# Softplus written to delta's buffer in SBUF, and DVE's product with u reading it there

## The chip, the cores and the metric

The kernel runs on one core of a Trainium2 chip. The metric is the device time of the whole program on that core, in microseconds. A core has five engines with queues of their own: PE (matmuls), DVE (VectorE), ACT (ScalarE), POOL (GpSimd) and SP, which here only issues DMAs. They meet at semaphores. PE writes only to PSUM; POOL works on SBUF alone.

## What is computed

Eight images of 96x64x64 go through a layer with a state-space block (two-dimensional selective scan), two convolutions with channel attention, an attention layer and a quantized feed-forward layer. Nearly all the time goes to the selective scan, with K = 4 directions, D_INNER = 192 channels, 16 states per channel and 4096 positions:

```python
def selective_scan(xs, dts, A, Bs, Cs, Ds, dt_bias):
    delta = jax.nn.softplus(dts + dt_bias[None, :, :, None])
    ...
    def step(h, inp):
        u_t, d_t, b_t, c_t = inp
        dA = jnp.exp(d_t[..., None] * A)
        h = dA * h + (d_t * u_t)[..., None] * b_t[:, :, None, :]
        y = jnp.einsum('bkdn,bkn->bkd', h, c_t)
        return (h, y)
    _, ys = jax.lax.scan(step, h0, (u_l, d_l, B_l, C_l))
    y = jnp.moveaxis(ys, 0, -1)
    return y + Ds[None, :, :, None] * xs
```

The change touches `delta` (the softplus) and `d_t * u_t`, its product with u, which the kernel calls `du`.

## The kernel before

For each of the eight images the program runs a stage that prepares the inputs (`prep`: norms, projections, depthwise convolution), the scan stage, and a stage for the rest (`post`). The scan stage takes about 1160 us of an image's 1530.

**How the scan is cut.** The 4 x 192 rows of channels are laid out as T = 0 to 5, each with 128 partitions: T = 0 and 3 walk the image by rows, T = 1 and 4 by columns, and T = 2 and 5 hold the remaining 64 channels of both ways. Each T has 4 chunks of 1024 positions. So an image has 24 chunks g, each with n = 0 to 15 steps, one for each state: 384 steps. All tiles of a step are 128x1024, f32. Below, "chunk (1, 2)" is T = 1 with its third chunk, counted from 0.

**A step**, engine by engine (the lines are those of the profile):

- ACT computes exp(delta * A) into `decay` (into a PSUM tile `pb` for n in `POOLED` = 3, 7, 11, 15), L1199, and copies the last column of a finished state into `carry`, L1143.
- DVE runs the scan, L1278, over 1024 positions. In 8 of 16 steps it first multiplies B, spread over the partitions in PSUM by PE (L1015), by `du`, L1265. In the 4 steps of `POOLED`, POOL makes that product from SBUF, L1298, and in the 4 steps of `TURNS` = 1, 5, 9, 13 ACT (L1186) and PE (L1056, transposes) do.
- POOL multiplies the state by C, L1309, in place; PE adds the sixteen up in PSUM, L1065. POOL has 16 + 4 instructions of 128x1024 in a chunk.

The order on each engine is written out by hand: each engine has a function `steps` that walks the steps of a chunk, with constants such as `SOFTPLUS_AT` that say behind which step the work for the following chunk stands. Every engine works through its queue in order.

**delta of the following chunk.** Within chunk g, PE computes the pre-activation of g + 1 into the PSUM tile `pc` after step 1 (`pre_dt`). ACT turns it into delta at step 2 (`softplus`, L1149, in place in `pc`, between two loads of ACT's tables). DVE reads `pc` and u at step 5 and writes `du` (`next_du`, L1245; L1283 is the same for the first chunk of a stage). At step 7 ACT copies `pc` to `delta` in SBUF (`delta_out`, L1157). Then `pc` is used again: PE turns B in it (`turn_b`, step 8, L1040), ACT takes that out, and PE turns `du` in it (`turn_du`, step 11, L1048). In chunks of T = 1 and 4, u is read by columns, with a stride of 64 elements (`chunk`).

`du` and `delta` have two buffers each, by the parity of g. All of `u`, `du`, `delta`, `decay`, `state`, `c_sb` and `b_sb` lie in SBUF; `pb`, `pc` and `py` in PSUM.

## Time and profile before

| | us |
|---|---|
| median of 3 runs (12321.95 to 12329.25) | 12322.18 |
| the profiled execution | 12312.74 |
| its span, first to last instruction | 12310.8 |
| DVE busy | 10864.5 (88%) |
| PE busy | 10629.6 (86%) |
| POOL busy | 9515.3 (77%) |
| ACT busy | 8817.2 (72%) |

The profile is of one execution. "Busy" is the time in which an engine has an instruction running; the shares are means over stages that differ: in the scan stage DVE and POOL are busy nearly all the time, and in `post` POOL has little to do. A view of groups gives, for each line of the kernel, how often its instruction ran, its mean duration, and how long the engine had sat idle just before it. A timeline gives single instructions with their start. Consecutive instructions of an engine overlap by 0.04 to 0.09 us in these records, so durations and starts are to be read together.

### The profile page before, as it was taken

To read this page: it belongs to the slowest core of one execution; us is meant where nothing else is said; L and a number is where in the kernel's file an instruction comes from. 1 tells how busy PE (TensorE), PEld (TensorE's weight loads), DVE (VectorE), ACT (ScalarE), POOL (GpSimd) and SP (SyncE) were. 2 spreads that over 40 slices of the span, in tenths; PEclk is the share of its full clock that TensorE was granted. 3 is DMA by queue.
4 is the path that set the end of the run, shared out by engine and by line. 5 is a ranking of instruction groups with operands and counts; after the bars stand their busy time and mean duration, and the time that the engine had idled before them with its cause. 6 is when DMAs were issued, how large, how long until landed. Compare 5 with 4: busy or idle time off the path is not lost. (4 is left out here: it accounts for less than half of the span.)

```text
span 12310.8 us, 117469 instructions
## 1 busy us (share of the span) xinstructions
PE 10629.6 (86%) x33046; PEld 4749.1 (39%) x33046; DVE 10864.5 (88%) x7695; ACT 8817.2 (72%) x18292; POOL 9515.3 (77%) x4213
## 2 busy tenths in 40 slices
PE   7888888888888888888888888888888888888888
PEld 2443334343344433434334443334433344334443
DVE  7999779997799978999789997899968999689996
ACT  5777667776677766777667776677766777667776
POOL 4999459994599945999459994599936999369993
PEclk9999989999899998999989999999998999999999
DMA  4677446764467644677446774477745677356773
GB/s 140 214 222 214 117 133 215 221 215 110 134 214 222 214 109 139 215 221 214 104 143 215 221 214 101 148 215 219 214 97 149 216 220 215 94 153 215 219 215 91
DMA packets 677497, 2203.72 MB, mean 179 GB/s; under 512 B 165008, under 2 KB 167056, under 8 KB 665424
## 3 DMA queue, kind: packets, MB, share of 16 engines
q1 hardware_dynamic: 676848, 2196.22, 61.3%
q8 instruction: 266, 4.36, 0.2%
q14 instruction: 383, 3.14, 0.1%
HBM read 2098.86 MB, written 67.11 MB: 176 GB/s over the span
## 5 line engine op out<-in xcount | busy, mean ns | idle before, releaser
L1309 POOL TENSOR_TENSOR state<-state,c_sb 128x1024 f32<-128x1024 f32 x3072 | 7180.7, 2363 | 610.5 <-ACT carry L1143 528.5
L1065 PE MATMUL ps<-state,wt 128*128 128x512 f32 x12288 | 5863.5, 614 | 350.5 <-ACT ya L1136 233.4
L1278 DVE TENSOR_TENSOR_SCAN state<-decay,carry,ps 128x1024 f32<-128x1024 f32 x1728 | 4006.7, 2340 | 41.1
L1065 PEld LDWEIGHTS ps<-state,wt 128*128 128x128 f32 x12288 | 2324.5, 196 | 2778.8 <-issue 2105.3
L1199 ACT ACTIVATE decay<-delta,a_neg 128x1024 f32<-128x1024 f32 x2304 | 2638.6, 1146 | 0.2 <-issue 0.2
L1186 ACT ACTIVATE dbu_t<-du_t,b_t 128x128 f32<-128x128 f32 (+1 forms) x8128 | 2301.4, 360 | 0.0
L1143 ACT COPY carry<-state 128x1 f32<-128x1 f32 x3072 | 572.0, 186 | 2136.4 <-DVE state L1278 2127.1
L1265 DVE TENSOR_TENSOR ps<-ps,du 128x1024 f32<-128x1024 f32 x1544 | 1866.2, 1209 | 97.9 <-PE ps L1015 97.6
L1298 POOL TENSOR_TENSOR dbu<-b_sb,du 128x1024 f32<-128x1024 f32 x768 | 1811.5, 2359 | 0.0
L1015 PE MATMUL ps<-parts,sel 114*128 114x512 bf16 (+1 forms) x3088 | 944.7, 388 | 679.6 <-DVE state L1278 673.1
L1278 DVE TENSOR_TENSOR_SCAN state<-ps,carry,dbu 128x1024 f32<-128x1024 f32 x576 | 1343.2, 2332 | 68.1 <-ACT ps L1199 47.6
L1278 DVE TENSOR_TENSOR_SCAN state<-decay,ps 128x1024 f32<-128x1024 f32 x576 | 1301.9, 2280 | 13.6
L1056 PE MATMUL ps<-wt,dbu_t 128*128 128x128 f32 x6080 | 812.5, 276 | 184.0 <-ACT dbu_t L1186 177.4
L1056 PEld LDWEIGHTS ps<-wt,dbu_t 128*128 128x128 f32 x6080 | 683.2, 141 | 627.6 <-issue 434.3
L1199 ACT ACTIVATE ps<-delta,a_neg 128x1024 f32<-128x1024 f32 x768 | 854.4, 1113 | 0.0
L1015 PEld LDWEIGHTS ps<-parts,sel 114*128 114x128 bf16 (+1 forms) x3088 | 218.6, 97 | 1529.4 <-DVE state L1278 1309.7
L1625 POOL CAST h<-h16b 128x1536 fp8e5<-128x1536 f16 x64 | 116.0, 1812 | 896.0 <-DVE h16b L1750 896.0
L307 ACT ACT_TABLE_LOAD x409 | 524.7, 1283 | 71.4 <-DMA x_tok<-x 27.1
L1278 DVE TENSOR_TENSOR_SCAN state<-ps,dbu 128x1024 f32<-128x1024 f32 x192 | 436.3, 2272 | 29.2 <-ACT ps L1199 16.0
L507 ACT ACTIVATE rs<-ps,wt 96x512 f32<-96x512 f32 (+1 forms) x320 | 218.7, 683 | 314.5 <-PE ps L492 171.9
L1611 POOL TENSOR_TENSOR sqa<-sqa,sqr 64x512 f32<-64x512 f32 x64 | 100.9, 1577 | 402.2 <-ACT sqr L1519 402.2
L1027 PE MATMUL ps<-parts,dt_w 114*128 114x512 bf16 (+1 forms) x1536 | 377.7, 389 | 30.3 <-PEq L664 30.3
(218 smaller groups left out, 9959.1 us busy)
## 6 DMA issues: line engine op xcount, KB each, us to landing
c_sb<-bc SPq DMA_DIRECT2D x2048, 512.0 KB, 4.6
c_sb<-bc SPq DMA_DIRECT2D x2048, 256.0 KB, 5.7
b_sb<-bc SPq DMA_DIRECT2D x512, 512.0 KB, 4.1
b_sb<-bc SPq DMA_DIRECT2D x512, 256.0 KB, 4.0
x_nat<-x SPq DMA_DIRECT2D x17, 1536.0 KB, 14.8
gates<-gate_a SPq DMA_DIRECT2D x8, 2048.0 KB, 6.8
x_tok<-x SPq DMA_DIRECT2D x288, 48.0 KB, 1.9
gn<-gn_t SPq DMA_DIRECT2D x8, 1536.0 KB, 7.1
```

Source lines behind the costliest of these rows:

```text
L307: act.add_instruction(mybir.InstLoadActFuncSet(name=nc.get_next_instruction_name(), act_func_set_id=which, ins=[], outs=[]))
L1015: mm = pe.matmul(bank[:, q * CH:(q + 1) * CH], sel[own, n, first:first + 128], part_cols(at, 2 * (T // 3), q, own), start=True, stop=True)
L1027: mm = pe.matmul(pc[:, q * CH:(q + 1) * CH], dt_w[own, p, w, :], part_cols(at, k, q, own), start=(i == 0 and p == 0), stop=(i == len(ways) ...
L1056: mm = pe.transpose(pb[n % 2][:, j * 128:(j + 1) * 128], dbu_t[:, j, :], col("ident"))
L1065: mm = pe.matmul(py[:, q * CH:(q + 1) * CH], col("ident"), state[:, slot(g, n), q * CH:(q + 1) * CH], start=(n == 0), stop=False)
L1143: act.copy(carry[:, n:n + 1], state[:, slot(g, n), last:last + 1]).then_inc(S["carried"], 1)
L1186: last = act.activation(dbu_t[:, j, o * wide:(o + 1) * wide], du_t[:, j, o * wide:(o + 1) * wide], ACT.Copy, scale=b_t[:, g % 2, j, i:i + 1])
L1199: act.activation(pb[n % 2][:, :] if n in POOLED else decay[:, n % 2, :], delta[:, g % 2, :], ACT.Exp, scale=a_neg[:, T, n:n + 1]).then_inc ...
L1265: dve.tensor_tensor(pb[n % 2][:, :], pb[n % 2][:, :], du[:, g % 2, :], ALU.mult)\
L1278: dve.tensor_tensor_scan(state[:, slot(g, n), way], rate, what, 0.0 if fresh else carry[:, n:n + 1], ALU.mult, ALU.add)\
L1298: pool.tensor_tensor(dbu[:, i % BRING, :], b_sb[:, i % BRING, :], du[:, g % 2, :], ALU.mult)\
L1309: pool.tensor_tensor(state[:, slot(g, n), :], state[:, slot(g, n), :], c_sb[:, n % CRING, :], ALU.mult).then_inc(S["weighted"], 1)
```

## The change

The softplus writes to `delta` in SBUF and no longer to `pc`; `next_du` reads `delta` there; `delta_out`, ACT's copy, and its semaphore `delta_ready` are gone. Who waited for `delta_ready` now waits for `delta_made`. The softplus waits for the readers of the buffer that it overwrites, two chunks back, and `turn_du` waits for `du_ready` itself.

```diff
@@ -1031,7 +1031,7 @@
                     def turn_b(T, at, g):
 
-                        pe.wait_ge(S["delta_ready"], g + 1)
+                        pe.wait_ge(S["delta_made"], g + 1)
...
@@ -1044,6 +1044,7 @@
                     def turn_du(g):
 
                         pe.wait_ge(S["bt_out"], g + 1)
+                        pe.wait_ge(S["du_ready"], g + 1)
...
@@ -1146,15 +1147,12 @@
 
                         tables(act, SOFTPLUS_SET)
                         act.wait_ge(S["pre_mm"], g + 1)
-                        act.activation(pc[:, :], pc[:, :], ACT.Softplus, bias=col("dt_b", 128, T))\
+                        if g > 1:
+                            act.wait_ge(S["decayed"], (g - 1) * NS)
+                            act.wait_ge(S["du_ready"], g - 1)
+                        act.activation(delta[:, g % 2, :], pc[:, :], ACT.Softplus, bias=col("dt_b", 128, T))\
                            .then_inc(S["delta_made"], 1)
                         ln_exp_tables(act)
-
-                    def delta_out(g):
-
-                        act.wait_ge(S["du_ready"], g + 1)
-                        act.wait_ge(S["decayed"], max(g - 1, 0) * NS)
-                        act.copy(delta[:, g % 2, :], pc[:, :]).then_inc(S["delta_ready"], 1)
...
@@ -1203,8 +1201,6 @@
                                 if n == SOFTPLUS_AT:
                                     softplus(following[0], g + 1)
-                                if n == DELTA_AT:
-                                    delta_out(g + 1)
...
                     softplus(0, 0)
-                    delta_out(0)
                     b_out(0, 0)
...
@@ -1242,7 +1237,7 @@
                         dve.wait_ge(S["dbu_pooled"], (g - 1) * NP + CREDIT)
                         if g > 1:
                             dve.wait_ge(S["dut_mm"], g - 1)
-                        dve.tensor_tensor(like(du[:, g % 2, :], T), like(pc[:, :], T), u_of(T, at), ALU.mult)\
+                        dve.tensor_tensor(like(du[:, g % 2, :], T), like(delta[:, g % 2, :], T), u_of(T, at), ALU.mult)\
                            .then_inc(S["du_ready"], 1)
...
                     dve.wait_ge(S["delta_made"], 1)
-                    dve.tensor_tensor(du[:, 0, :], pc[:, :], u_of(0, 0), ALU.mult).then_inc(S["du_ready"], 1)
+                    dve.tensor_tensor(du[:, 0, :], delta[:, 0, :], u_of(0, 0), ALU.mult).then_inc(S["du_ready"], 1)
```

ACT's queue at the head of a scan stage, before the change: L1149 is the softplus, L1157 the copy to `delta`, L1163 takes the turned B out of `pc`, L1172 the turned `du`, L1199 is the first exponential.

```order
L307 ACT_TABLE_LOAD
L1149 ACTIVATE ps<-ps,wt 128x1024
L307 ACT_TABLE_LOAD
L1157 COPY delta<-ps 128x1024
L1163 COPY b_t<-ps 128x8x4
L1172 COPY du_t<-ps 128x1024
L1199 ACTIVATE decay<-delta,a_neg 128x1024 x2
```

And after it:

```order
L307 ACT_TABLE_LOAD
L1153 ACTIVATE delta<-ps,wt 128x1024
L307 ACT_TABLE_LOAD
L1161 COPY b_t<-ps 128x8x4
L1170 COPY du_t<-ps 128x1024
L1197 ACTIVATE decay<-delta,a_neg 128x1024 x2
```

The copy between the second table load and the copy of B is gone; in the same way it goes from behind step 7 of each later chunk, with nothing else moved.

DVE's queue in the first chunk, from step 3 to step 6, before (scans are printed with the operation's other name; `du` of the following chunk is L1245):

```order
L1278 SCALAR_TENSOR_TENSOR state<-ps,dbu 128x1024
L1265 TENSOR_TENSOR ps<-ps,du 128x1024
L1278 SCALAR_TENSOR_TENSOR state<-decay,ps 128x1024
L1245 TENSOR_TENSOR du<-ps,ua 128x1024
L1278 SCALAR_TENSOR_TENSOR state<-decay,ps 128x1024
```

And after:

```order
L1273 SCALAR_TENSOR_TENSOR state<-ps,dbu 128x1024
L1260 TENSOR_TENSOR ps<-ps,du 128x1024
L1273 SCALAR_TENSOR_TENSOR state<-decay,ps 128x1024
L1240 TENSOR_TENSOR du<-delta,ua 128x1024
L1273 SCALAR_TENSOR_TENSOR state<-decay,ps 128x1024
```

Nothing moves here; the product has the same place, and its first input is `delta` in SBUF where it was a tile of PSUM.

## Rows read from the trace of the kernel before

**Rows 1.** Page, costliest groups: busy, mean ns, idle before, and its causes

```profile
L1278 DVE TENSOR_TENSOR_SCAN state<-decay,carry,ps 128x1024 f32<-128x1024 f32 x1728 | 4006.7, 2340 | 41.1
```

**Rows 2.** Busy time by engine, scan stage of the second image, T = 0

```profile
core 0: us, PE busy (x) PEld busy (x) DVE busy (x) ACT busy (x) POOL busy (x), PEclk, DMA share, GB/s
1725.00:1905.00 180.00, 156.84 (x498) 68.07 (x498) 176.13 (x95) 131.93 (x266) 172.56 (x75) 0.92 0.67 217
```

**Rows 3.** The product `du`, whole program: duration ns min/median/max, first and last start

```profile
L1245 DVE TENSOR_TENSOR du<-ps,ua x120: 1198/1898/1943, 207.6 to 11805.6; 128x1024 f32<-128x1024 f32 x120
L1245 DVE TENSOR_TENSOR du<-ps,ur x64: 1201/1225/1226, 546.3 to 12001.2; 128x1024 f32<-128x1024 f32 x64
```

**Rows 4.** Timeline of `post`, DVE and POOL: start us, us, instruction [idle before]

```profile
1374.42 0.74 DVE L1650 SCALAR_TENSOR_TENSOR ya<-ya,wt,gate_a 128x512 f32<-128x512 f32 x1
1374.43 1.85 POOL L1611 TENSOR_TENSOR sqa<-sqa,sqr 64x512 f32<-64x512 f32 x1 [5.01 <-ACT sqr L1519]
1375.09 1.74 DVE L1653 SCALAR_TENSOR_TENSOR yrc<-yrc,wt,gate_r 64x512 f32<-64x512 f32 x1
...
1381.28 1.82 DVE L1641 SCALAR_TENSOR_TENSOR yrc<-yrc,wt,rs 64x512 f32<-64x512 f32 x1
1381.29 1.25 POOL L1611 TENSOR_TENSOR sqa<-sqa,sqr 64x512 f32<-64x512 f32 x1 [5.01 <-ACT sqr L1519]
```

**Rows 5.** Timeline of `prep`, the end of POOL's share of the convolution

```profile
121.68 1.27 POOL L720 TENSOR_TENSOR conv_acc<-conv_acc,conv_tap 128x512 f32<-128x512 f32 x1
...
122.77 0.49 DVE L848 TENSOR_SCALAR conv_acc<-pad_r,wt 128x512 f32<-128x512 f32 x1
...
123.04 1.35 POOL L720 TENSOR_TENSOR conv_acc<-conv_acc,conv_tap 128x512 f32<-128x512 f32 x1
```

**Rows 6.** Timeline, five chunks of the second image: POOL's instruction and DVE's `du`

```profile
1783.45 2.34 POOL L1309 TENSOR_TENSOR state<-state,c_sb 128x1024 f32<-128x1024 f32 x1
1785.18 1.20 DVE L1245 TENSOR_TENSOR du<-ps,ua 128x1024 f32<-128x1024 f32 x1
...
1830.76 2.34 POOL L1309 TENSOR_TENSOR state<-state,c_sb 128x1024 f32<-128x1024 f32 x1
1832.93 1.20 DVE L1245 TENSOR_TENSOR du<-ps,ua 128x1024 f32<-128x1024 f32 x1
...
2026.05 2.37 POOL L1309 TENSOR_TENSOR state<-state,c_sb 128x1024 f32<-128x1024 f32 x1 [0.18 <-ACT carry L1143]
2026.07 1.93 DVE L1245 TENSOR_TENSOR du<-ps,ua 128x1024 f32<-128x1024 f32 x1 [0.32 <-PE ps L1056]
...
2074.94 2.36 POOL L1309 TENSOR_TENSOR state<-state,c_sb 128x1024 f32<-128x1024 f32 x1 [0.19 <-ACT carry L1143]
2075.53 1.23 DVE L1245 TENSOR_TENSOR du<-ps,ur 128x1024 f32<-128x1024 f32 x1 [0.89 <-PE ps L1056]
...
2171.82 2.36 POOL L1309 TENSOR_TENSOR state<-state,c_sb 128x1024 f32<-128x1024 f32 x1 [0.57 <-ACT carry L1143]
2172.91 1.23 DVE L1245 TENSOR_TENSOR du<-ps,ur 128x1024 f32<-128x1024 f32 x1
```

**Rows 7.** Waits of the program (us in total, times, longest); POOL at a step 8

```profile
POOL state L1309 <- ACT carry L1143: 528.5, 457, 30.8
...
1942.44 2.35 POOL L1309 TENSOR_TENSOR state<-state,c_sb 128x1024 f32<-128x1024 f32 x1 [0.93 <-ACT carry L1143]
```

**Rows 8.** Timeline, head of the second image's scan stage: ACT, DVE and PE

```profile
1713.67 1.09 ACT L1149 ACTIVATE ps<-ps,wt 128x1024 f32<-128x1024 f32 x1 [0.56 <-PE ps L1027]
...
1714.79 1.23 DVE L1283 TENSOR_TENSOR du<-ps,ua 128x1024 f32<-128x1024 f32 x1 [3.38 <-ACT ps L1149]
...
1716.07 1.01 ACT L1157 COPY delta<-ps 128x1024 f32<-128x1024 f32 x1
...
1717.78 1.97 PE L1048 MATMUL ps<-wt,du 128*128 128x128 f32 x8 [0.28 <-ACT b_t L1163]
```

**Rows 9.** DVE with two inputs in SBUF, and with one in PSUM: ns min/median/max

```profile
L514 DVE TENSOR_TENSOR cen<-cen,rs x128: 671/679/689, 59.3 to 12184.2; 96x512 f32<-96x512 f32 x128
...
L497 DVE TENSOR_TENSOR cen<-x,ps x192: 669/682/685, 1386.2 to 12288.6; 96x512 f32<-96x512 f32 x192
```

More of the change, by code:

```diff
@@ L66 @@
 BLOCKS = 8
-PRE_AT, SOFTPLUS_AT, DU_AT, DELTA_AT = 1, 2, 5, 7
+PRE_AT, SOFTPLUS_AT, DU_AT = 1, 2, 5
 BT_AT, BT_OUT_AT, DUT_AT, DUT_OUT_AT = 8, 10, 11, 13
@@ L277, in build @@
         gn_stored gates_ready gates_stored conv_mm conv_taps u_ready conv_r conv_p conv_sum ur_ready
-        ur_in xp_mm xp_hi xp_out xp_rest xp_mid xp_low parts_zero bc_stored parts_in pre_mm delta_made delta_ready du_ready b_mm decayed dbu_ready
+        ur_in xp_mm xp_hi xp_out xp_rest xp_mid xp_low parts_zero bc_stored parts_in pre_mm delta_made du_ready b_mm decayed dbu_ready
         dbu_pooled scanned carried weighted summed y_summed y_taken c_in_0 c_in_1 c_in_2 c_in_3 b_in_0
@@ L1196, in steps @@
                             if n == 0:
-                                act.wait_ge(S["delta_ready"], g + 1)
+                                act.wait_ge(S["delta_made"], g + 1)
                             act.wait_ge(S["scanned"], g * NS + n - 1 + CREDIT)
```

## The prediction

> **What bounds the kernel now.** I read the page's groups first. DVE's scans are the largest work that must run in order: 1728 of the 3072 take 2340 ns each, and DVE sat idle before them for 41.1 us in the whole program [rows 1]. So in the scan stage DVE is the engine that sets the time. The table by stretch says it again and adds the second thing to see: of 180 us, DVE is busy 176.13 and POOL 172.56 [rows 2]. POOL is only 3.6 us behind DVE, its instructions follow each other nearly without a gap, and any moment at which DVE starts something finds POOL in the middle of an instruction. ACT (131.93) and PE are not the bound [rows 2]. Whatever is added to DVE's queue in the scan stage comes out at the end; what is taken from ACT there does not, unless DVE was waiting for ACT.
>
> The third view is where the change has its cost: what happens when a DVE instruction with both inputs in SBUF meets a POOL instruction. In the scan stage of before there is none: each product, scan and `du` has one input in PSUM. In `post` there is. At 1374.42 DVE starts L1650, both inputs in SBUF, and POOL's L1611 starts 0.01 us behind it. POOL takes 1.85 us, where the same instruction takes 1.25 at 1381.29 [rows 4]: it was held for 0.60, the time in which DVE streamed its 512 elements. Then DVE's L1653 starts at 1375.09, beneath POOL's instruction, and takes 1.74 us where its twin L1650 took 0.74. It ends at 1376.83, 0.55 after POOL's end at 1376.28. At 1381.28 the same once more: L1641 takes 1.82, ending at 1383.10, 0.56 behind POOL's end at 1382.54 [rows 4]. So the two do not share: the later waits until the earlier is through. For 512 elements, 0.55 us is about the streaming alone (0.74 less some 0.18 of start, which lay under POOL's tail).
>
> The Trainium skill has the rule, in "SBUF — State Buffer", section "Who interferes with whom": a DVE instruction with two SBUF inputs reads the second through an interface that it shares with GpSimd, and whichever comes second blocks fully. The trace agrees (1.74 for 0.74).
>
> **The change, part by part.**
>
> *1. `du` from SBUF.* 184 products [rows 3] (23 per image; the first of each stage, L1283, comes when POOL has nothing to do) now have two SBUF inputs, in the middle of POOL's work. Each pays what is left of POOL's current instruction, less a start-up of about 0.12 us (0.68 of an instruction of this kind [rows 9], less the 0.55 that is left of it behind POOL's end [rows 4]). The remainder can be read off, since each chunk of a kind meets POOL in nearly the same phase. From the timeline of the second image, POOL's start plus its time less DVE's start:
> - 3 chunks per image, (1, 1), (1, 2) and (4, 2): both start together, 2026.05 + 2.37 - 2026.07 = 2.35 us [rows 6];
> - 2 chunks, (1, 3) and (4, 3): 2074.94 + 2.36 - 2075.53 = 1.77;
> - 5 chunks, (2, 1) to (2, 3), (5, 1) and (5, 2): 2171.82 + 2.36 - 2172.91 = 1.27;
> - 5 chunks, (0, 1), (2, 0), (3, 0), (3, 1), (5, 0): 0.32 to 0.61, mean 0.46; the 0.61 is 1783.45 + 2.34 - 1785.18;
> - 7 chunks, (0, 2), (0, 3), (1, 0), (3, 2), (3, 3), (4, 0), (4, 1): 0.16 to 0.31, mean 0.21; 1830.76 + 2.34 - 1832.93 = 0.17;
> - 1 chunk, (0, 0): POOL idle, nothing.
>
> Sum: 3 x 2.35 + 2 x 1.77 + 5 x 1.27 + 5 x 0.46 + 7 x 0.21 = 7.05 + 3.54 + 6.35 + 2.30 + 1.47 = 20.7; less 22 x 0.12 = 2.6 gives 18.1 us per image, **145 us** in eight. It is on the path: behind `du` stand scan 5 and all later steps on DVE, and no wait follows that it could fill (see 3).
>
> Does POOL's next instruction, right behind the current one, get in first? The nearest row is in `prep`: DVE's L848 starts at 122.77 under a POOL instruction that ends at 122.95. POOL's next, which follows at once, starts at 123.04 and takes 1.35 in place of 1.27, and DVE is through at 123.26 [rows 5]. So DVE came in between two adjoining POOL instructions. I take one wait per product, not two.
>
> *2. The product itself.* SBUF in place of PSUM: 679 ns with both inputs in SBUF, 682 with one in PSUM [rows 9]. Taken at 0. For T = 1 and 4 the 1.90 us come from reading u by columns [rows 3], which stays. Another page of the Trainium skill, "VectorE: DVE Perf Modes", section on the TRN2 errata, gives a fixed 120 cycles to a PSUM source and 58 to an SBUF one; as an estimate from it, 0.065 us x 184 would be 12 us less. The rows show 3 ns, so it is not in my sum.
>
> *3. POOL held.* While DVE streams, POOL stands: about 1.08 us (1.20 less 0.12) for 15 products of an image, and 1.8 for the 8 with a stride. But DVE has lost the remainder too, so relative to DVE POOL falls back by 1.08 less the remainder: ahead at 1.27, back 0.9 at 0.17, and 1.6 in the strided chunks with a short remainder. POOL waits for ACT's carry 528.5 us in the program, of which the openings of eight stages are 30 each [rows 7]: 290 us in 192 chunks, 1.5 in each, mostly at steps 6 and 8, soon after `du` (0.93 at one step 8 [rows 7]). That covers it, and because POOL meets DVE again at step 8, the phases above should come back in the next chunk. Taken at 0; if that cover is gone, POOL's 15 x 1.08 + 8 x 1.8 = 31 us per image is the price, 245 in all, less the 145 that DVE pays already.
> Late in chunks of T = 2 and 5 DVE waits a little for POOL and PE, which now have had more time. Between 0 and 20 us; I take **-7**.
>
> *4. The copy goes.* 1.01 us of ACT [rows 8], 184 times in the loop. ACT has 48 of 180 us free [rows 2] and waits there for DVE's scans: 0. At the head of a stage it is on the path: ACT's copy from 1716.07 to 1717.08, then PE's `turn_b`, ACT's copy of B, and `turn_du` at 1717.78 [rows 8]. Now `turn_b` runs on PE under the table load, `du` ends at 1716.02, and `turn_du` can start near 1716.3. That is 1.45 us (between 1.01, the copy, and 1.75), eight times: **-12**.
>
> *5. The softplus.* It reads PSUM and writes SBUF; the copy L1157 does that in 1.01, the softplus into PSUM takes 1.09 [rows 8]. Between -0.08 and +0.08 on a piece of ACT's queue for which DVE waits at step 3: 15 us at most either way, taken at 0. Its new waits are for work a chunk back and long done; `turn_du`'s wait for `du_ready`, at step 11, is for step 5. PE's and SP's queues don't move.
>
> Sum: 145 - 7 - 12 = +126 us. On the profiled execution, 12312.7 + 126 = 12439; the median lies 9.4 above that execution, so 12448.
>
> **The rivals.**
> - *Ties fall to DVE.* In the three chunks with 2.35 us both engines start within 0.02 us. Of the pairs in rows 4, DVE had the earlier start both times, won one and lost one. If DVE wins these: 3 x 2.2 x 8 = 53 us less, 12395. Still slower.
> - *The phases drift, or POOL becomes the bound.* If POOL's hold shifts it so that DVE meets it at random, the remainder is half of 2.34, 1.17 less 0.12, times 184: 193 us; if half of POOL's hold that DVE has not paid comes on top, some 50: up to 12322 + 240 = 12562. For it: POOL has 1.5 us of slack against a hold of 1.8 in the strided chunks. Against: it waits at both steps 6 and 8 there.
> - *POOL's next instruction does get in first.* Then each of the 10 longest cases per image pays 2.3 more, 184 us: about 12630. Rows 5 speak against it; there DVE's instruction is of another kind, though.
> - *No conflict* (faster or level, the other side of the forecast): the block is for the pair in `post`, or the second input of this `tensor_tensor` isn't read through what POOL uses. Then only the head's 12 us, and up to 15 of the softplus, are left: 12295 to 12320, at 12308 within 0.2%. It decides at one place, `du`'s duration beside a POOL instruction: 1.20 or up to 3.5 us. Rows 4 speak against it plainly, with instructions that read SBUF as both do here.
>
> **How the numbers follow.** Forecast as worked out, the ties either way: 0.65. Drift or POOL as bound: 0.15. Two waits per product: 0.05. No conflict: 0.15, of which a quarter ends faster by over 0.2%. A measurement of this kernel can tell about 0.2% (25 us) from no change, so: faster 0.04, same 0.12, slower 0.84. Range: from 12370, below the ties' 12395 for the term of the softplus, to 12565, the drifting case's end; outside lie the case without conflict and the one with two waits, 0.2.
>
> **What would show it.** In the profile of the changed kernel: `du` (now L1240) takes 1.20 to 3.5 us for an unstrided input, mean about 0.8 above before's, and ends some 1.1 us (1.8 strided) behind the end of the POOL instruction that it met. POOL's instruction behind it takes up to 1.1 or 1.8 us longer or starts later. Scan 5 follows at once. The copy of 1.01 us is gone from ACT and ACT's idle time grows by as much. The first scan of a stage comes about 1.45 us earlier. If `du` stays at 1.20 and 1.90 everywhere, step 1 is wrong; if it is right but the total is off by over 50 us, step 3 is (phases, POOL's slack): POOL's wait at step 8 would have gone.

## The result, and the profile after

The changed kernel takes **12474.85 us** (median, 12463.19 to 12493.39), the kernel before 12322.11 (12321.95 to 12329.25): a ratio of 1.0124, 95% interval 1.0106 to 1.0141, so 1.2% slower. The forecast was 12448, from 12370 to 12565. The profiled executions are 12463.19 and 12312.74 us long, their spans 12461.3 and 12310.8: 150.5 us more.

Nearly all of it stands in the busy time of one instruction. The view of groups, kernel after (line, engine, operation, count, busy us, mean ns, idle before and its cause):

```profile
L1240 DVE TENSOR_TENSOR du<-delta,ua 128x1024 f32<-128x1024 f32 x120 | 273.1, 2276 | 11.8 <-PE ps L1057 11.8
L1240 DVE TENSOR_TENSOR du<-delta,ur 128x1024 f32<-128x1024 f32 x64 | 145.4, 2273 | 35.1 <-PE ps L1057 33.6
```

The same groups of the kernel before:

```profile
L1245 DVE TENSOR_TENSOR du<-ps,ua 128x1024 f32<-128x1024 f32 x120 | 190.2, 1585 | 12.5 <-PE ps L1056 12.5
L1245 DVE TENSOR_TENSOR du<-ps,ur 128x1024 f32<-128x1024 f32 x64 | 78.4, 1224 | 35.1 <-PE ps L1056 33.9
```

273.1 + 145.4 less 190.2 + 78.4 is 149.9 us. In single instructions (min/median/max ns), where [rows 3] had 1198/1898/1943 and 1201/1225/1226:

```profile
L1240 DVE TENSOR_TENSOR du<-delta,ua x120: 1199/1930/6553, 206.5 to 11949.8; 128x1024 f32<-128x1024 f32 x120
L1240 DVE TENSOR_TENSOR du<-delta,ur x64: 1515/2352/2885, 552.2 to 12148.5; 128x1024 f32<-128x1024 f32 x64
```

The page says how little else moved. The scan takes 2340 ns as before and DVE's idle time before it is 48.5 us (41.1 in [rows 1]). POOL's L1304 now waits 461.5 us for the carry (528.5 in [rows 7]), and its instructions take 2416 ns on average, with the times in which they are held:

```profile
L1304 POOL TENSOR_TENSOR state<-state,c_sb 128x1024 f32<-128x1024 f32 x3072 | 7344.5, 2416 | 566.0 <-ACT carry L1144 461.5
...
L1273 DVE TENSOR_TENSOR_SCAN state<-decay,carry,ps 128x1024 f32<-128x1024 f32 x1728 | 4007.8, 2340 | 48.5 <-PE ps L1057 7.4
```

ACT is busy 8650.2 us by the page, instead of 8817.2: the copies are gone, and nobody was waiting for them. In the table by stretch for T = 0 of the second image, which answers to [rows 2], DVE remains the engine with nearly no idle time (175 of 180 us):

```profile
1745.00:1925.00 180.00, 150.54 (x476) 65.03 (x477) 175.06 (x91) 123.41 (x253) 168.11 (x72) 0.92 0.66 210
```

**How one product waits.** The timeline of the second image, for the chunks of [rows 6]: start, duration, engine, instruction, idle time before. The first DVE row in each piece is `du`, the POOL row beside it is the instruction that it met, the next POOL row the one behind.

```profile
1858.55 1.26 DVE L1240 TENSOR_TENSOR du<-delta,ua 128x1024 f32<-128x1024 f32 x1
...
1856.38 2.34 POOL L1304 TENSOR_TENSOR state<-state,c_sb 128x1024 f32<-128x1024 f32 x1
...
2104.16 2.88 DVE L1240 TENSOR_TENSOR du<-delta,ur 128x1024 f32<-128x1024 f32 x1 [0.87 <-PE ps L1057]
...
2103.60 2.36 POOL L1304 TENSOR_TENSOR state<-state,c_sb 128x1024 f32<-128x1024 f32 x1 [0.17 <-ACT carry L1144]
...
2203.53 2.35 DVE L1240 TENSOR_TENSOR du<-delta,ur 128x1024 f32<-128x1024 f32 x1
...
2202.44 2.36 POOL L1304 TENSOR_TENSOR state<-state,c_sb 128x1024 f32<-128x1024 f32 x1 [0.68 <-ACT carry L1144]
...
2204.76 3.32 POOL L1304 TENSOR_TENSOR state<-state,c_sb 128x1024 f32<-128x1024 f32 x1
```

Read the third, chunk (2, 1). POOL's instruction ends at 2204.80, 1.27 us after `du` starts. `du` ends at 2205.88, 1.08 behind that, so of its 2.35 us 1.14 were waiting. POOL's next starts in the records at 2204.76, takes 3.32 in place of 2.36, and ends when it would have ended had it begun behind `du`'s reading. In chunk (1, 3) 1.80 is left and `du` takes 2.88 (1.08 behind POOL's end again); in (0, 2) 0.17 is left and it takes 1.26.

Two pieces are not of that form. In chunk (1, 1) both start together (POOL at 2003.62, for 2.37 us), and POOL was first: `du` takes 4.13, its normal 1.92 and 2.21 of waiting. In (1, 2) both start together, and DVE was first: `du` takes its normal 1.92, and POOL's instruction 4.13.

```profile
2003.63 4.13 DVE L1240 TENSOR_TENSOR du<-delta,ua 128x1024 f32<-128x1024 f32 x1 [0.31 <-PE ps L1057]
...
2054.72 1.92 DVE L1240 TENSOR_TENSOR du<-delta,ua 128x1024 f32<-128x1024 f32 x1 [0.29 <-PE ps L1057]
...
2054.72 4.13 POOL L1304 TENSOR_TENSOR state<-state,c_sb 128x1024 f32<-128x1024 f32 x1 [0.17 <-ACT carry L1144]
```

And in chunk (0, 1) `du` takes 6.25 us. With 0.57 of POOL's instruction left it lets not only that one go by, but the two behind it, and gets in only when POOL has nothing more to do:

```profile
1804.41 6.25 DVE L1240 TENSOR_TENSOR du<-delta,ua 128x1024 f32<-128x1024 f32 x1
...
1802.63 2.35 POOL L1304 TENSOR_TENSOR state<-state,c_sb 128x1024 f32<-128x1024 f32 x1
...
1804.93 2.35 POOL L1304 TENSOR_TENSOR state<-state,c_sb 128x1024 f32<-128x1024 f32 x1
...
1807.24 2.34 POOL L1293 TENSOR_TENSOR dbu<-b_sb,du 128x1024 f32<-128x1024 f32 x1
```

I call this a lost turn below: a POOL instruction that began after `du` had, and read first.

### The profile page after: what moved, and what is told of

Its sections match the earlier page's. It is cut to its first block and busy times, and to the rows that moved or that the text cites. A ratio compares the mean times of both kernels' runs of the same rounds, so it can differ in the third digit from the quotient of the medians.

```text
span 12461.3 us, 117445 instructions
## 1 busy us (share of the span) xinstructions
PE 10691.9 (86%) x33046; PEld 4774.9 (38%) x33046; DVE 11017.6 (88%) x7695; ACT 8650.2 (69%) x18100; POOL 9711.9 (78%) x4213
## 5 line engine op out<-in xcount | busy, mean ns | idle before, releaser
L1304 POOL TENSOR_TENSOR state<-state,c_sb 128x1024 f32<-128x1024 f32 x3072 | 7344.5, 2416 | 566.0 <-ACT carry L1144 461.5
L1066 PE MATMUL ps<-state,wt 128*128 128x512 f32 x12288 | 5916.8, 618 | 350.6 <-ACT ya L1137 233.7
L1273 DVE TENSOR_TENSOR_SCAN state<-decay,carry,ps 128x1024 f32<-128x1024 f32 x1728 | 4007.8, 2340 | 48.5 <-PE ps L1057 7.4
L1066 PEld LDWEIGHTS ps<-state,wt 128*128 128x128 f32 x12288 | 2344.4, 197 | 2803.3 <-issue 2123.9
L1293 POOL TENSOR_TENSOR dbu<-b_sb,du 128x1024 f32<-128x1024 f32 x768 | 1839.7, 2395 | 0.0
L1015 PE MATMUL ps<-parts,sel 114*128 114x512 bf16 (+1 forms) x3088 | 954.1, 391 | 792.5 <-DVE state L1273 788.3
L1057 PE MATMUL ps<-wt,dbu_t 128*128 128x128 f32 x6080 | 819.2, 277 | 168.9 <-ACT dbu_t L1184 163.4
L1057 PEld LDWEIGHTS ps<-wt,dbu_t 128*128 128x128 f32 x6080 | 689.0, 142 | 612.1 <-issue 414.0
L1015 PEld LDWEIGHTS ps<-parts,sel 114*128 114x128 bf16 (+1 forms) x3088 | 219.6, 98 | 1644.9 <-DVE state L1273 1415.0
```

What stands on the lines that cost most here:

```text
L1015: mm = pe.matmul(bank[:, q * CH:(q + 1) * CH], sel[own, n, first:first + 128], part_cols(at, 2 * (T // 3), q, own), start=True, stop=True)
L1057: mm = pe.transpose(pb[n % 2][:, j * 128:(j + 1) * 128], dbu_t[:, j, :], col("ident"))
L1066: mm = pe.matmul(py[:, q * CH:(q + 1) * CH], col("ident"), state[:, slot(g, n), q * CH:(q + 1) * CH], start=(n == 0), stop=False)
L1273: dve.tensor_tensor_scan(state[:, slot(g, n), way], rate, what, 0.0 if fresh else carry[:, n:n + 1], ALU.mult, ALU.add)\
L1293: pool.tensor_tensor(dbu[:, i % BRING, :], b_sb[:, i % BRING, :], du[:, g % 2, :], ALU.mult)\
L1304: pool.tensor_tensor(state[:, slot(g, n), :], state[:, slot(g, n), :], c_sb[:, n % CRING, :], ALU.mult).then_inc(S["weighted"], 1)
```

## The experiments

The question was whether the 150 us are what the prediction says: `du` pays, from SBUF and only from SBUF, what is left of POOL's instruction at the place where it meets it.

### The same order with one input moved: PSUM against SBUF

The first pair has the same instructions at the same places and differs in one operand. In both, ACT's copy of delta stands at step 5, `du` behind it at step 6. Two waits follow from that order, in both alike: the first product of a stage now waits for ACT's copy, and `turn_b` waits for `du`. The kernel is otherwise the one before. In the first `du` reads `pc` in PSUM, in the second `delta` in SBUF.

```diff
-PRE_AT, SOFTPLUS_AT, DU_AT, DELTA_AT = 1, 2, 5, 7
+PRE_AT, SOFTPLUS_AT, DU_AT, DELTA_AT = 1, 2, 6, 5
...
-                        act.wait_ge(S["du_ready"], g + 1)
+                        act.wait_ge(S["delta_made"], g + 1)
...
-                        dve.wait_ge(S["delta_made"], g + 1)
+                        dve.wait_ge(S["delta_ready"], g + 1)
```

and in the second also:

```diff
-                        dve.tensor_tensor(like(du[:, g % 2, :], T), like(pc[:, :], T), u_of(T, at), ALU.mult)\
+                        dve.tensor_tensor(like(du[:, g % 2, :], T), like(delta[:, g % 2, :], T), u_of(T, at), ALU.mult)\
```

> The kernel before with two moves: ACT's copy of delta to SBUF at step 5 (it was at 7), and du at step 6 (it was at 5), still with pc in PSUM as its first input. Partner of e2_sbuf_at6, which differs from it in that input alone. Theory (a DVE instruction with two SBUF inputs and a POOL instruction exclude each other): du takes 1.20 to 1.23 us, and 1.9 with the stride, in all 184 cases; the time is that of the kernel before but for what the moved copy costs DVE: 12310 to 12360 us. Rival (what costs time in the changed kernel is the earlier or moved work on ACT, or du's place): this kernel is slower than before by 100 us or more.

> As e1_psum_at6, with delta in SBUF as the first input of du, and nothing else changed (the same waits, the same copy on ACT). Theory: each du pays the rest of POOL's running instruction less 0.12 us. At step 6 of the trace of before that rest sums to 226 us over the 184 products (phases taken as they were with du at step 5; ties and POOL getting in first can add or take 50): 150 to 280 us over e1_psum_at6. Rival (the second SBUF input costs nothing; something else of the change does): within 25 us of e1_psum_at6. Second rival (the cost does not hang on POOL's phase but is a fixed price of the operand): 150 us, and du longer by the same amount in every chunk.

From PSUM: 12363.71 us (12344.9 to 12366.77), ratio to the kernel before 1.003 (1.0017 to 1.0042). From SBUF: 12597.58 (12590.65 to 12609.26), ratio 1.0224 (1.0209 to 1.024). Groups of `du`, from PSUM and then from SBUF:

```profile
L1248 DVE TENSOR_TENSOR du<-ps,ua 128x1024 f32<-128x1024 f32 x120 | 193.3, 1610 | 4.2
L1248 DVE TENSOR_TENSOR du<-ps,ur 128x1024 f32<-128x1024 f32 x64 | 78.4, 1224 | 2.2
```

```profile
L1248 DVE TENSOR_TENSOR du<-delta,ua 128x1024 f32<-128x1024 f32 x120 | 387.2, 3226 | 4.2
L1248 DVE TENSOR_TENSOR du<-delta,ur 128x1024 f32<-128x1024 f32 x64 | 109.8, 1715 | 2.2
```

The one operand costs 233.9 us in the medians and 497.0 - 271.7 = 225.3 us in `du`'s busy time. The same chunk, (0, 2) of the second image, in the timelines of the two:

```profile
1845.57 1.22 DVE L1248 TENSOR_TENSOR du<-ps,ua 128x1024 f32<-128x1024 f32 x1
...
1844.79 2.35 POOL L1301 TENSOR_TENSOR dbu<-b_sb,du 128x1024 f32<-128x1024 f32 x1
```

```profile
1882.45 2.65 DVE L1248 TENSOR_TENSOR du<-delta,ua 128x1024 f32<-128x1024 f32 x1
...
1881.65 2.36 POOL L1301 TENSOR_TENSOR dbu<-b_sb,du 128x1024 f32<-128x1024 f32 x1
...
1883.97 3.33 POOL L1312 TENSOR_TENSOR state<-state,c_sb 128x1024 f32<-128x1024 f32 x1
```

Both meet POOL's instruction with 1.57 and 1.56 us left. From PSUM `du` takes 1.22; from SBUF 2.65, and POOL's next is held to 3.33. So the second SBUF input is the cause, with nothing else changed (the first product of each stage reads the other source too, but POOL is idle there). The change under study does two things at once, since it also drops the copy; this pair has the copy in both. The remainders in the second kernel's own trace, each less 0.12, sum to 184 us, and 22 of its 184 products lost one turn, some 50 us more: 234 us together, against the 229 by which `du` is longer than undisturbed products are.

The first kernel came out 3.7 us above the upper end of what was expected of it. In it DVE waits 36 us more for others. 20 of them are at the head of the eight stages, where the first product waits for ACT's copy, 49.8 us in all, and had waited 29.6 for the softplus:

```profile
L1286 DVE TENSOR_TENSOR du<-ps,ua 128x1024 f32<-128x1024 f32 x8 | 9.8, 1224 | 49.8 <-ACT delta L1160 49.8
```

The rest is for PE: 14 us more for its sum (23.1 at L1066, where the kernel before has 8.8) and 12 more for its B (109.6 at L1015, where it has 97.6), with some 10 less elsewhere. That is a first sign that `du`'s place matters to more than the meeting with POOL.

### du at other steps

If each product pays the remainder at its place, the place sets the price. One line of the changed kernel is edited, with 4, 9 and 10 in turn:

```diff
-                    PRE_AT, SOFTPLUS_AT, DU_AT = 1, 2, 5
+                    PRE_AT, SOFTPLUS_AT, DU_AT = 1, 2, 9
```

> The changed kernel with du at step 9 (it was at 5), which is free now since pc is no longer held for it. At step 8 POOL waits for the carry in most chunks, so DVE finds it idle. Theory (the price of du is the rest of POOL's running instruction): read off the trace of before at step 9 the rests sum to 36 us; with du gone from step 5 POOL has 1.1 to 1.8 us less slack up to step 8, which gives some of it back. 12320 to 12400 us, and du's excess over 1.21 and 1.92 us sums to what the kernel has over 12310. Rival (a fixed price per product, or POOL's hold of 245 us is what costs): no better than the changed kernel, 12450 to 12490.

> The changed kernel with du at step 10, one step further. There POOL has just begun an instruction in nearly all chunks: the rests in the trace of before sum to 283 us. Theory: 12310 + 283 = 12590, 12530 to 12640, the slowest of all places so far although the code differs from e_du9 by one step. Rival (no dependence on POOL's phase): as e_du9 within 25 us.

> The changed kernel with du at step 4 (it was at 5). Theory: the rests of POOL's instruction at step 4 of the traces sum to 75 us (148 at step 5); and du now stands ahead of DVE's wait for the turned product of step 5, which is 56 us in the program and can take some of it in. 12310 + 75 - 56 = 12330, with the phases' uncertainty 12310 to 12400. Rival (a fixed price per product): 12450 less at most 56, 12395 to 12450. du's excess would tell: 60 to 110 us in sum against 150.

Measured: at 9 12513.89 us (12503.52 to 12529.81), ratio 1.0157 (1.014 to 1.0173); at 10 12805.62 (12780.01 to 12813.42), ratio 1.0389 (1.037 to 1.0407); at 4 12570.06 (12563.18 to 12578.33), ratio 1.0196 (1.0181 to 1.0211). All three totals were missed, every one by being slower. What `du` itself costs came as expected at 10 (283 us expected, 273 measured); at 9 the 36 us that had been read off became 68, and at 4 the 60 to 110 became 137. By its total the kernel with `du` at 9 came out as its rival had it, no better than the change; but the rival's reason, a fixed price per product, is ruled out by `du`'s own 68, 150 and 273 us at three places. Groups of `du`, at step 9 and then at step 10:

```profile
L1240 DVE TENSOR_TENSOR du<-delta,ua 128x1024 f32<-128x1024 f32 x120 | 232.0, 1933 | 0.0
L1240 DVE TENSOR_TENSOR du<-delta,ur 128x1024 f32<-128x1024 f32 x64 | 104.7, 1636 | 0.0
```

```profile
L1240 DVE TENSOR_TENSOR du<-delta,ua 128x1024 f32<-128x1024 f32 x120 | 381.1, 3176 | 4.2
L1240 DVE TENSOR_TENSOR du<-delta,ur 128x1024 f32<-128x1024 f32 x64 | 160.5, 2509 | 2.2
```

At 9 `du` is busy 336.7 us, at 10 541.6, against 268.6 in the kernel before: 68 and 273 us more, where the change has 150. The remainders of their own traces, less 0.12 each, sum to 64 and 259 us, the rest is lost turns (two in one product at 9, one each in eight products at 10). At 4 they sum to 69, but 30 products lost a turn, which makes 137. The account of DVE's time in the scan stage shows where the totals went. "Waits" is all that `du`, the products with B and the scans waited for other engines, summed over DVE's rows in the view of waits; the differences are to the kernel before (268.6 and 270.4 us, span 12310.8):

| `du` at | `du` busy | waits | sum | span |
|---|---|---|---|---|
| 5, the change | +150.0 | -1.5 | +148.5 | +150.5 |
| 9 | +68.1 | +104.9 | +173.0 | +190.9 |
| 10 | +273.1 | +191.1 | +464.2 | +500.8 |
| 4 | +136.5 | +104.6 | +241.1 | +257.5 |
| 6, PSUM | +3.0 | +35.8 | +38.8 | +51.5 |
| 6, SBUF | +228.3 | +36.3 | +264.6 | +278.0 |

The last two rows agree in their waits: these belong to the order (some 20 us to the head, as said above, the rest to the place) and not to the source. The sum leaves 2 to 37 us of the span's difference that I have not assigned. Who is waited for: DVE's waits (us in total, times, longest) with `du` at 9,

```profile
DVE ps L1260 <- PE ps L1015: 120.0, 121, 3.3
...
DVE state L1273 <- PE ps L1057: 106.7, 134, 2.8
...
DVE state L1273 <- PE ps L1066: 36.2, 48, 1.3
```

with `du` at 10, and PE's there,

```profile
DVE state L1273 <- PE ps L1057: 190.1, 187, 2.6
```

```profile
PE ps L1049 <- DVE du L1240: 362.6, 183, 4.4
```

and with `du` at 4:

```profile
DVE ps L1260 <- PE ps L1015: 132.2, 154, 3.3
DVE state L1273 <- PE ps L1066: 94.4, 125, 1.5
```

In the changed kernel the waits at L1015, L1057 (in scans) and L1066 are 84.0, 7.4 and 7.4. With `du` at 10, PE stands at `turn_du` (L1049, step 11) until `du` is there, 183 times, and what it owes DVE at step 13 comes late: 145 us of the 190.1 are there. With `du` at 9 that wait of PE is gone (2.7 us in all), yet by single records DVE waits 63 us at step 13, where it had waited next to nothing; the cause of that part stays open. The wait at step 5 is no part of the price: the wait for PE's turned product stands ahead of `du` in DVE's queue, and it is 45.3 us in the changed kernel (in `du`) and 43.5 with `du` at 9 (in the scan). What `du` at step 5 did cover lies behind it: at steps 7 and 8, PE's sum and PE's B cost 29 and 23 us more without it there. With `du` at 4, ahead of the wait at step 5, that wait is gone, and 87 us more for PE's sum and 33 for ACT's exponential at step 7, and 43 more for B at step 8, take its place. I had worked out the remainders only and taken PE as a cover that stays.

**The clock of TensorE moves too.** PE runs at one of two levels, 2.4 GHz, or 1.2 where a profile's PEclk reads 0.50; a matmul of L1066 takes 592 ns at the one and 1061 at the other (medians). In the scan stages the traces have 551 us at the lower level in the kernel before, 733 in the changed one, and 834, 1192 and 1226 with `du` at 9, 10 and 4. In the last, the second image has, besides 31 us at its head, such a stretch of 3.4 to 10.2 us in nearly every chunk. In one of them the clock fell just as PE came out of a wait of 2.46 us for ACT's copy of the finished sum, and DVE's scan at step 7 then waited 1.24 us for the sum:

```profile
2124.00:2127.00 3.00, 3.00 (x4) 1.12 (x4) 2.35 (x1) 2.50 (x7) 3.00 (x2) 0.50 0.14 52
...
2127.61 2.35 DVE L1273 TENSOR_TENSOR_SCAN state<-ps,carry,dbu 128x1024 f32<-128x1024 f32 x1 [1.24 <-PE ps L1066]
```

Of the 105 us more that DVE waits with `du` at 4, 78 are waits that ended at the lower level; with `du` at 9 and 10 it is 10 of 105 and 15 of 191. So at 4 the place and the clock cannot be told apart by these runs; at 9 and 10 little of what is waited stands in those stretches. In the changed kernel the waits that ended at the lower level are 62 us, where the kernel before has 73: the clock has no visible part in the 150.

### du at step 3 from PSUM, with the new head

Here the kernel before takes over only the head of the change: ahead of the first chunk the softplus goes to `delta`, and the first `du` reads it there. `du` of the other chunks, from PSUM, moves to step 3, where DVE waits 0.56 us on average for ACT's exponential in 113 of 192 chunks.

```diff
-PRE_AT, SOFTPLUS_AT, DU_AT, DELTA_AT = 1, 2, 5, 7
+PRE_AT, SOFTPLUS_AT, DU_AT, DELTA_AT = 1, 2, 3, 7
...
-                    softplus(0, 0)
-                    delta_out(0)
+                    act.sem_inc(S["delta_ready"], 1)
+                    tables(act, SOFTPLUS_SET)
+                    act.wait_ge(S["pre_mm"], 1)
+                    act.activation(delta[:, 0, :], pc[:, :], ACT.Softplus, bias=col("dt_b", 128, 0))\
+                       .then_inc(S["delta_made"], 1)
+                    ln_exp_tables(act)
...
-                    dve.tensor_tensor(du[:, 0, :], pc[:, :], u_of(0, 0), ALU.mult).then_inc(S["du_ready"], 1)
+                    dve.tensor_tensor(du[:, 0, :], delta[:, 0, :], u_of(0, 0), ALU.mult).then_inc(S["du_ready"], 1)
```

> A version that should beat both. The kernel before (du reads pc in PSUM, the copy at step 7 stays) with du at step 3, where DVE waits for the exponential that follows the softplus (79 us in the program at step 3, and 56 at step 5), and with the changed kernel's order at the head of a stage alone (softplus to delta, du reading it there, no copy; POOL is idle then): -12. Theory: du's 1.2 us go into those waits: up to -120, and the head -12: 12190. But in e_du9, where du was also gone from step 5, DVE waited some 0.5 us more per chunk for PE at steps 7 and 8; if that comes here too, 60 to 100 comes back. 12200 to 12300. Rival (PE is the bound behind step 5 and takes all of it): 12300 to 12330.

12339.49 us (12324.17 to 12346.39), ratio 1.0008 (0.9999 to 1.0017): no gain. DVE's waits for other engines, where the kernel before has 63.6 for ACT's L1199 at step 3, 46.4 for PE in `du`, and 8.8 for PE's sum:

```profile
DVE ps L1272 <- PE ps L1015: 106.6, 135, 3.3
DVE state L1285 <- PE ps L1067: 102.0, 115, 1.5
```

The wait at step 3 is gone entirely, and PE's sum at step 7 takes its place. What is saved ahead of that is handed back there. 58 of the 102 us are again waits that ended with PE at its lower clock (908 us of it in the scan stages, 551 in the kernel before). This is the rival that the expectation named, a few microseconds worse; whether PE's place or its clock is what hands the gain back was not separated.

### The new head alone

```diff
-                    softplus(0, 0)
-                    delta_out(0)
+                    act.sem_inc(S["delta_ready"], 1)
...
```

with the other lines of the head as above and `du` at step 5 from PSUM.

> The kernel before with the new head alone: before the first chunk of each image ScalarE's softplus goes straight to delta's buffer and the first product with u reads it there, so that the copy of delta is no longer ahead of TensorE's first transposes and matmuls; all other chunks keep softplus in PSUM and ScalarE's copy. This is the prediction's step 4 by itself. In the changed kernel the first product of an image follows du by 1.47 us less than before, 8 times, 11.8 us. If that is a gain and nothing behind it takes it back: 12305 to 12316, the ratio about 0.999, with DVE's time in du unchanged at about 269 us, since no other product of an image reads SBUF twice. If what comes behind (POOL's state products, which the first chunk waits for at its step 11) is the bound of the first chunk, it is taken back in that wait: 12318 to 12326 and longer waits of the scan at step 11.

12320.89 us (12311.24 to 12335.78) against 12327.8 (12318.01 to 12342.49) for the kernel before beside it: ratio 0.9993, interval 0.9985 to 1.0002. The sign is the expected one, the size (6.9 us of the 11.8) cannot be told from nothing. `du` stayed at 268.8 us (268.6). The head is shorter, as in the changed kernel; but the scan at step 11 of the first chunk, which waits for POOL, waits longer: 1.25 us instead of 0.73, by the gaps between DVE's records in the eight images, so about 4 of the 12 us come back there. Even this best version is not shown to beat the kernel before.

### Inputs exchanged

Does it matter which of the two SBUF inputs comes second?

```diff
-                        dve.tensor_tensor(like(du[:, g % 2, :], T), like(delta[:, g % 2, :], T), u_of(T, at), ALU.mult)\
+                        dve.tensor_tensor(like(du[:, g % 2, :], T), u_of(T, at), like(delta[:, g % 2, :], T), ALU.mult)\
```

> The changed kernel with the product's inputs exchanged: u first, delta second. If any second SBUF input excludes POOL whichever it is, du's excess is 150 us as in the changed kernel and the time 12460 to 12490. If it mattered which tile comes second (its address or its stride), the strided chunks of T = 1 and 4 would differ from the others, or the excess go away.

12461.89 us (12454.5 to 12472.91), ratio 1.0109 (1.0092 to 1.0126). The groups of `du`:

```profile
L1240 DVE TENSOR_TENSOR du<-ua,delta 128x1024 f32<-128x1024 f32 x120 | 265.5, 2212 | 11.4 <-PE ps L1057 11.4
L1240 DVE TENSOR_TENSOR du<-ur,delta 128x1024 f32<-128x1024 f32 x64 | 145.4, 2273 | 34.3 <-PE ps L1057 32.5
```

The same to the tenth of a microsecond for `ur`, and 8 us less for `ua`. There the three ties of an image fell to DVE in 24 of 24 cases here, in 19 of 24 in the changed kernel. And the strided products that wait only for a short remainder are 0.06 to 0.08 us shorter: 1.90 instead of 1.98 in chunk (0, 3), with 0.19 and 0.18 left. So the order of the inputs takes nothing off the wait that is worth having.

### Does a lost turn hang on the moment or on the chunk?

In the changed kernel chunk (0, 1) lost two turns in 7 of 8 images, with 0.56 to 0.61 us of POOL's instruction left, and (3, 0) two in one image, at 0.60. A fill by DVE, ahead of `du`, moves the moment: first of 128x128 in all chunks of T = 0 and 3, then of 128x480 in chunk (0, 1) alone.

```diff
+                            if n == DU_AT and after and T in (0, 3):
+                                dve.memset(idle_out[:, :], 0.0)
```

```diff
+                            if n == DU_AT and after and (T, c) == (0, 1):
+                                dve.memset(idle_out[:, :], 0.0)
```

> The changed kernel with a memset of 128x128, about 0.2 us, put on DVE ahead of du in the 8 chunks of T = 0 and 3 of each image. In the changed kernel the du of chunk (0, 1), which starts 0.56 to 0.61 us before the end of POOL's instruction, lost to POOL twice in 7 of 8 images and took 6.3 us; at 0.48 it was never lost, nor at 1.27. If the loss hangs on the moment, it goes: (0, 1) takes 1.2 + 0.3 us, some 4 us less per image, and the memset itself costs nothing where it shortens the wait by as much: 12322 + 150 - 31, 12420 to 12460. If it hangs on the chunk (its addresses, its queue), (0, 1) stays at 6.3 us and the time at 12470 to 12500.

> The changed kernel with one more fill of 128x480 values by DVE, ahead of the du that is executed in the second chunk of transform 0 alone (8 times in all). There du took 6.2 to 6.3 us in 8 of 8 images, with 0.46 of POOL's instruction left as well as with 0.60. The fill of 128x128 moved du by 0.14 us; this one should move it by about 0.5 us, so that it starts within 0.15 us of the end of POOL's instruction. If the two lost turns belong to starts with 0.4 to 0.6 us left: du takes about 1.3 us there and the whole is 8 x (5.07 - 0.5) = 37 us less than the changed kernel, 12430 to 12445. If they belong to this chunk, whatever the moment: du still takes 5.8 to 6.2 us and the time is 12465 to 12480. If du then comes after POOL's next one has begun: about 3.6 us for du, 12445 to 12460.

The first: 12479.77 us (12473.43 to 12489.88), ratio 1.0123 (1.0108 to 1.0138). The second: 12487.47 (12475.03 to 12509.48), ratio 1.0126 (1.011 to 1.0141). Chunk (0, 1) of the second image in the two timelines:

```profile
1816.17 6.16 DVE L1241 TENSOR_TENSOR du<-delta,ua 128x1024 f32<-128x1024 f32 x1
...
1814.27 2.36 POOL L1307 TENSOR_TENSOR state<-state,c_sb 128x1024 f32<-128x1024 f32 x1
```

```profile
1821.02 0.46 DVE L1266 MEMSET idle_out<- 128x480 f32 x1
1821.40 5.78 DVE L1241 TENSOR_TENSOR du<-delta,ua 128x1024 f32<-128x1024 f32 x1
...
1819.11 2.38 POOL L1307 TENSOR_TENSOR state<-state,c_sb 128x1024 f32<-128x1024 f32 x1
...
1821.42 2.37 POOL L1307 TENSOR_TENSOR state<-state,c_sb 128x1024 f32<-128x1024 f32 x1
...
1823.73 2.37 POOL L1296 TENSOR_TENSOR dbu<-b_sb,du 128x1024 f32<-128x1024 f32 x1
```

0.46 and 0.09 us are left now, and the two turns are lost in 8 of 8 images in both, as expected if the chunk decides (the second total is 7 us above the range for that case); `du` ends at the same place behind POOL's third instruction. In the changed kernel products that meet POOL with 0.44 to 0.48 left, in (2, 0), (3, 1) and (5, 0), lose none; with the first fill (3, 1) lost two turns in one image. So the moment alone does not decide. Nor does the chunk alone: (3, 0) and (3, 1) lose two turns in single images (both in one image with the second fill, with 0.76 and 0.53 left), and none in the others.

## Why the prediction came out as it did

**Step 1, the remainder of POOL's instruction: right by mechanism; that the sum fits so well is in part luck.** 145 us forecast, 150 measured. The price per product is the remainder less 0.12 to 0.13 us: 1.14 at 1.27, 1.67 at 1.80, 0.32 at 0.45, 0.05 at 0.18. The phases of before held almost exactly (1.77 became 1.80, 1.27 stayed). The pair from PSUM and from SBUF shows the source to be the cause, and three other places show the price to follow the place.

The rule of the Trainium skill that I leaned on, in "SBUF — State Buffer", section "Who interferes with whom", is borne out: full waiting, either way round. In chunk (2, 1) POOL was held 0.96 us (3.32 for 2.36) and DVE 1.14.

**But the sum holds two errors that cancel.**
- *The ties.* 3 chunks per image were priced at 2.23 us each, 53 us in all. They cost 0.56, 0.55 and 0.28 on average, 11 us: DVE won 19 of 24. That was the first rival, and taken alone it happened: 42 us less.
- *One wait per product.* The prediction drew this from one row of `prep` [rows 5], with another kind of DVE instruction. It failed in 12 products besides the ties: (0, 1) in 7 of 8 images, with 5.07 us extra where 0.49 was forecast, (3, 0) once, (4, 1) in 4 of 8, with 2.3 or 4.6 extra at a remainder of 0.10 to 0.14. Over what was forecast for those three chunks that is 48 us. That is the rival of the two waits, in 12 of 184 products instead of 80.

145 - 42 + 48 = 151. That is luck: a sum that fits to 4% had two terms that were each off by more than 40 us; only the durations of single chunks show it.

**Step 2, the product itself: right.** Where POOL leaves it alone it takes 1.199 us from SBUF, 1.198 from PSUM [rows 3]. The 12 us less of the estimate from the Trainium skill, "VectorE: DVE Perf Modes", did not come; the prediction had left them out of its sum.

**Step 3, POOL held, covered by its slack: right.** POOL's wait for the carry fell from 528.5 to 461.5 us, DVE's waits for POOL's product rose only from 23.5 to 26.6, and all waits of DVE together changed by -1.5. The -7 taken for late waits did not come: the scans waited 12.0 us more for others, 7.4 of it for PE's L1057, 3.1 for POOL, 2.9 for ACT, and 1.4 less for PE's sum. No drift: the phases are those of before, but for (3, 0), which lies anywhere from 0.31 to 0.77 us in the kernel before, too.

**Step 4, the copy: right in the head, less in the total.** In the head of the second image (ACT, DVE, PE):

```profile
1734.59 1.11 ACT L1153 ACTIVATE delta<-ps,wt 128x1024 f32<-128x1024 f32 x1 [0.62 <-PE ps L1027]
1735.74 1.22 DVE L1278 TENSOR_TENSOR du<-delta,ua 128x1024 f32<-128x1024 f32 x1 [3.46 <-ACT delta L1153]
...
1737.26 1.97 PE L1049 MATMUL ps<-wt,du 128*128 128x128 f32 x8 [1.12 <-ACT b_t L1161]
```

From the start of `du` to `turn_du` it is 1737.26 - 1735.74 = 1.52 us, where it was 2.99 [rows 8]: 1.47 less, against 1.45 forecast. The wait of the products for PE's L1015, which holds the head, fell from 97.6 to 84.0 us. In the total it does not appear, because the scans' 12.0 us of step 3 are against it: `du`'s 150.0 account for the 150.5 alone. The kernel with the head alone gained 6.9 us, not told from nothing. The loop's 184 copies were worth nothing, as said.

**Step 5, the softplus into SBUF: right.** Its mean is 1114 ns instead of 1088, 5 us over the program, on an engine that is not waited for much there (66.5 us at step 3 instead of 63.6).

So the forecast was 27 us low, 0.2%. The late waits are most of it, 19 us between the -7 forecast and the +12 measured; step 1 was low by 5, and 2 are that the median lies farther above the profiled execution (11.7 us instead of 9.4).

## What to carry to other kernels

A DVE instruction in a loop in which POOL never rests should take one input from PSUM: it costs the same 1.20 us, and it doesn't meet POOL at all. Before an operand moves to SBUF, read off at each place of the loop how much of POOL's running instruction is left when DVE's starts; that, less about 0.12 us, is the price where no turn is lost, and another step with less left is a gain only if the instruction at its old place covered no wait for another engine. That wait has to be looked for at the later steps, with the clock that TensorE was granted there. And a term that is saved on an engine nobody waits for (167 us of ACT here) pays for nothing.

## What the runs showed of the hardware that I had not expected

- **A waiting DVE instruction can lose its turn to POOL's next ones.** In chunk (0, 1) `du` let two POOL instructions pass which began 0.52 and 2.83 us after it, took 6.25 us for 1.2, and came in when POOL had nothing left to run; the prediction had named 3.5 as the longest. Over the changed kernel's trace, with 0.25 to 2.3 us left: of 44 products that met POOL in a run without a pause 8 lost, of 68 whose POOL instruction had itself begun after a pause none did.
- **Every product that lost a turn had a POOL instruction behind that was free to start.** The records of ACT's copies into `carry` and of the DMAs' landings tell when POOL's next instruction was released. In the eight traces with `du` from SBUF, of the products that began 0.05 to 2.3 us before the end of POOL's instruction, 353 had a next one that was released less than 0.1 us before that end, or later: none lost a turn. All 116 that lost one had a next one released earlier (by 0.14 us at the least). Where the one behind it was not yet released, with `du` at 4, at 6 and at 10, all 58 lost one turn; in chunk (0, 1) both were, and it lost two (in (4, 1), where they were too, one or two). This is read off the records, and no run was made to test it. It does not say which products lose: in the changed kernel 85 of 97 with a released one behind still won, and (0, 1) loses with 0.60, 0.46 and 0.09 us left alike. What singles that chunk out stays open.
- **Ties are decided either way.** In the three chunks in which both start together, within 0.03 us, DVE won 19 of 24 in one kernel and 24 of 24 in one whose product differs only in the order of its inputs. In (4, 1), where POOL's next starts 0.03 to 0.09 us behind `du`, DVE won 4 of 8 in both. The loser pays in full: 2.2 us for DVE, 1.8 for POOL (4.13 for 2.36) under a strided product.
- **The order of a DVE product's two SBUF inputs makes next to no difference** to the wait (145.4 us for 64 products both ways; up to 0.08 us in a strided one).
